# Keys and values of the second attention prepared in earlier stages, idle products in TensorE's waits, and a shorter clearing of mask rows

## The reference

```python
x = x + _L0_xattn_ref(_layernorm(x), ctx, ctx, mask, ...)     # attention
x = x + _L0_ffn_ref(_layernorm(x), ...)                       # mixture of experts
x = x + _L1_xattn_ref(ctx, _layernorm(x))                     # alignment by dynamic time warping
x = x + _L1_ffn_ref(_layernorm(x), ...)                       # gated, int weights
x = x + _L2_xattn_ref(_layernorm(x), ctx, Wq, Wkv, Wo)        # attention with rotary positions
x = x + _L2_ffn_ref(_layernorm(x), ...)                       # mixture of experts
x = x + _L3_xattn_ref(_layernorm(x), ctx, ctx, ..., 32)       # attention over the 32 largest scores
x = x + _L3_ffn_ref(_layernorm(x), g_info, ...)               # attention in two groups of tokens

def _rope(x):                     # in _L2_xattn_ref, on q and k
    ...
    x_rot = jnp.stack([-x[..., 1::2], x[..., 0::2]], axis=-1).reshape(x.shape)
    return x * cos + x_rot * sin
```

## Time and profile before

| | |
|---|---|
| median of 3 runs | 2571.38 us (2570.29 to 2576.07) |
| the profiled execution | 2571.94 us, its span 2570.2 us |
| busy | PE 2017.0 us (78%), DVE 1667.7 (65%), ACT 1114.9 (43%), POOL 1014.1 (39%) |
| stages, us | l0a 218.02, l0f 236.38, dtw 305.84, l1f 150.56, l2a 226.47, l2f 363.53, l3a 786.12, l3g 48.01, l3f 235.27 |
| l2a alone, busy | PE 154.17, DVE 157.64, ACT 86.78, POOL 104.14 |

### The profile page before, as it was taken

How to read it: one execution, slowest core, us unless ns; L and a number is a source line. 1 busy time by engine, 2 the same in 40 slices (tenths; PEclk the granted TensorE clock), 3 DMA queues, 4 the chain that set the end, 5 groups by cost and what they waited for, 6 DMA issues and landing times. The chain is left out here.

```text
span 2570.2 us, 39975 instructions
## 1 busy us (share of the span) xinstructions
PE 2017.0 (78%) x13076; PEld 1627.1 (63%) x13076; DVE 1667.7 (65%) x5397; ACT 1114.9 (43%) x3119; POOL 1014.1 (39%) x954
## 2 busy tenths in 40 slices
PE   7985898699659948865999937777777777756996
PEld 5664797599538835545999925555655555544664
DVE  5765111588972258843111179999999999976774
ACT  3552232455221115432333236666666766652443
POOL 3310453200000046503555436666666666634440
PEclk9996899655769979976999966666666757567998
DMA  2111565400210012123364230000000000000111
GB/s 91 64 55 60 215 242 183 127 21 1 82 37 1 1 46 71 59 71 134 131 211 157 85 113 9 1 9 9 1 9 9 1 1 1 1 7 26 46 55 66
DMA packets 91715, 161.09 MB, mean 63 GB/s; under 512 B 18494, under 2 KB 69847, under 8 KB 83543
## 3 DMA queue, kind: packets, MB, share of 16 engines
q0 software_dynamic: 23808, 85.50, 9.6%
q1 hardware_dynamic: 67704, 73.06, 9.0%
HBM read 194.38 MB, written 33.33 MB: 89 GB/s over the span
## 5 line engine op out<-in xcount | busy, mean ns | idle before, releaser
L555 DVE MATCH_REPLACE8 l3a_left<-l3a_top,l3a_left 128x256 f32<-128x256 f32 x768 | 307.4, 406 | 0.0
L548 DVE MAX8 l3a_top<-l3a_left 128x8 f32<-128x256 f32 x768 | 284.6, 411 | 0.0
L365 POOL TENSOR_TENSOR l3a_prob<-l3a_expd,l3a_rest 128x512 f32<-128x512 f32 x128 | 162.4, 1269 | 234.1 <-ACT l3a_rest L445 233.9
L270 PE MATMUL l3a_psT<-all_ident,l3a_prob 128*128 128x128 f32 x512 | 123.5, 387 | 162.7 <-POOL l3a_prob L365 162.7
L288 PE MATMUL l3a_psO<-l3a_probT,l3a_vp 128*128 128x128 f32 x1024 | 218.4, 380 | 28.8 <-ACT l3a_probT L461 28.8
L288 PEld LDWEIGHTS l3a_psO<-l3a_probT,l3a_vp 128*128 128x128 f32 x1024 | 187.7, 274 | 82.6 <-ACT l3a_probT L461 47.7
L270 PEld LDWEIGHTS l3a_psT<-all_ident,l3a_prob 128*128 128x128 f32 x512 | 83.9, 196 | 185.9 <-POOL l3a_prob L365 185.5
L445 ACT ACTIVATE l3a_rest<-l3a_left,l3a_nmax 128x256 f32<-128x256 f32 x256 | 116.1, 502 | 153.2 <-DVE l3a_left L555 152.5
L1485 ACT ACTIVATE l2f_hT<-l2f_psH,l2f_wt 128x128 f32<-128x128 f32 x312 | 89.0, 368 | 215.5 <-PE l2f_psH L1417 215.5
L352 POOL TENSOR_TENSOR l3a_kept<-l3a_raw_sc,l3a_mone 128x512 f32<-128x512 f32 x128 | 163.0, 1274 | 46.3 <-ACT l3a_raw_sc L429 45.8
L949 POOL TENSOR_SCALAR l2a_xn<-all_x,l2a_nmean,all_rstd 128x256 f32<-128x256 f32 x16 | 8.7, 554 | 433.3 <-DVE all_rstd L106 433.3
(11 more groups left out here) (533 smaller groups left out, 4723.9 us busy)
## 6 DMA issues: line engine op xcount, KB each, us to landing
o_at<-l0a_oraw SPq DMA_DIRECT2D x16, 256.0 KB, 2.0
l0a_osum<-o_at SPq DMA_DIRECT2D x32, 128.0 KB
kv_at<-dtw_kv SPq DMA_DIRECT2D x8, 512.0 KB, 2.8
o_at<-l2a_oraw SPq DMA_DIRECT2D x16, 256.0 KB, 2.0
l2a_osum<-o_at SPq DMA_DIRECT2D x32, 128.0 KB
l2f_yb<-rows_y SPq DMA_DIRECT2D x8, 512.0 KB, 7.3
o_at<-l3f_oraw SPq DMA_DIRECT2D x16, 256.0 KB, 2.0
l3f_osum<-o_at SPq DMA_DIRECT2D x32, 128.0 KB
```

What stands on the lines that cost most here:

```text
L270: mm = nc.tensor.transpose(psT[u % 2][:, kc, e, :], prob[:, u % 4, e, kc * P:kc * P + P], ident[:])
L365: nc.gpsimd.tensor_tensor(prob[:, u % 4, :, :], expd[:, u % 2, :, :], rest[:, u % 2, :, :], ALU.subtract).then_inc(picked, 1)
L548: ins = nc.vector.max(top[:, e, eight], rows[:, e, :] if r else scores[:, e, :])
L555: ins = nc.vector.match_replace(out=rows[:, e, :], in_to_replace=top[:, e, eight], in_values=rows[:, e, :] if r else scores[:, e, :], imm_ ...
```

## The change

- alignment (dtw) makes three products per batch: keys, keys with the columns of each pair exchanged (a third weight, the key weight with its columns permuted), and values. ACT writes the values straight between the ones of a vd buffer that POOL filled once. Keys and exchanged keys go to k_at (512 KB a batch), values with ones to the second half of kv_at (512 KB).
- gated_ffn (l1f): GpSimd loads both keys, multiplies them by cosine and sine, adds, makes the two parted copies and stores them in the first half of kv_at: five instructions a batch.
- l2a loads each batch's parted keys into k2 and values into vd, three buffers each, both 512 KB. load(b) for b of 3 and more stands ahead of realign(2(b - 2)). DVE exchanges q alone and copies no values; POOL turns and parts q alone; the memset of vd is gone there.
- keep_busy writes n idle products of the identity with 512 columns into a bank that is not yet in use, in front of a wait of PE: 2 + 2 in the head of l0a and l2a, 4 ahead of l2a's first scores, 1 before the last values and 8 before the last output product of l0a, l2a and l3f, 4 in each moe, 2 + 1 in l1f, 1 + 3 in l3g: 54 in all.
- stats.root(act, 1) stands behind read_q(0) and read_k(0). In l0a and l3f the memset of vd stands ahead of the second moments.
- find_groups: POOL clears one row set of 128x2048, and ACT copies it to the four parts of mrow, two ahead of its second root and two at its end.

The diff, cut to its core:

```diff
+def keep_busy(nc, out, ident, n):
+    for _ in range(n):
+        nc.tensor.matmul(out, ident[:], ident[:].unsqueeze(1).to_broadcast([P, 4, P]), start=True, stop=True)
...
                 if kv_at is not None:
-                    if b >= 2:
-                        sp.wait_ge(k2_set, b - 1)
-                        sp.wait_ge(v_ev, b - 1)
-                    of = kv_at[b].rearrange("p (w c n) -> p w c n", w=2, c=DC)
-                    sp.dma_start(kf[:, b % 2, :, :], of[:, 0]).then_inc(kv_in[b % 2], 16)
-                    sp.dma_start(vraw[:, b % 2, :, :], of[:, 1]).then_inc(kv_in[b % 2], 16)
+                    if b >= 3:
+                        sp.wait_ge(s2_done, 16 * (b - 2))
+                        sp.wait_ge(pv_ps, 2 * (b - 2))
+                    sp.dma_start(k2[:, b % 3, :, :, :].rearrange("p e c n -> p (e c n)"), kv_at[b, :, 0:4 * S]).then_inc(kv_in[b % 3], 16)
+                    sp.dma_start(vd[:, b % 3, :, :, :].rearrange("p t h m -> p (t h m)"), kv_at[b, :, 4 * S:]).then_inc(kv_in[b % 3], 16)
                     return
...
                 load(2)
+            if given and kv_at is None:
                 load(3)
             for y in range(2 * B):
-                if given and y % 2 == 0 and y // 2 + 4 < B:
+                if given and kv_at is None and y % 2 == 0 and y // 2 + 4 < B:
                     load(y // 2 + 4)
+                if kv_at is not None and y % 2 == 0 and 3 <= y // 2 + 2 < B:
+                    load(y // 2 + 2)
                 realign(y)
...
             def scores_1(n):
                 b, c, qt = n // 4, n % 4 // 2, n % 2
+                out = [take("s1", 4 * n + j) for j in range(4)]
+                if n == 0 and rope is not None:
+                    busy(out[0], 4)
                 if n % 4 == 0:
                     pe.wait_ge(qd_set, b + 1)
-                    pe.wait_ge(k2_set, b + 1)
-                out = [take("s1", 4 * n + j) for j in range(4)]
+                    if kv_at is None:
+                        pe.wait_ge(k2_set, b + 1)
+                    else:
+                        pe.wait_ge(kv_in[b % 3], 32 * (b // 3 + 1))
                 for e in (1, 0):
                     for j in range(4):
...
                 b, c = y // 2, y % 2
                 out = take("pv", y)
+                if y == 2 * B - 1:
+                    busy(out, 1)
                 pe.wait_ge(exp_done, 8 * (y + 1))
-                if c == 0:
...
             def out_project(b):
                 out = take("out", b)
+                if b == B - 1:
+                    busy(out, 8)
...
             q_parted(0)
-            k_parted(0)
+            if kv_at is None:
+                k_parted(0)
...
             read_x(0)
-            if stats is not None:
-                stats.root(act, 1)
             read_q(0)
             if kv_at is None:
                 read_k(0)
+            if stats is not None:
+                stats.root(act, 1)
...
+                nc.vector.memset(vd[:].rearrange("p b k h m -> p (b k h m)"), 1.0).then_inc(vd_one, 1)
+                dve.wait_ge(vd_one, 1)
             if x_in is not None:
                 dve.wait_ge(x_in[1], x_in[2])
             if stats is not None:
                 stats.moments(dve, 1)
-            nc.vector.memset(vd[:].rearrange("p b k h m -> p (b k h m)"), 1.0).then_inc(vd_one, 1)
-            dve.wait_ge(vd_one, 1)
             dve.wait_ge(q_in, 16 * n_q)
             if rope is not None:
-                exchange(0, 0, qf, q_ev, q_shuf, q_sin, q_turn)
...
             dve.wait_ge(w_in, 16 * n_w)
-            read_v(0)
+            if kv_at is None:
+                read_v(0)
...
                 if rope is not None and t == 1 and b + 1 < B:
-                    exchange(b + 1, 0, qf, q_ev, q_shuf, q_sin, q_turn)
-                if rope is not None and t == 2 and b + 1 < B:
-                    exchange(b + 1, 1, kf, k_ev if kv_at is None else None, k_shuf, k_sin, k_turn)
+                    exchange(b + 1)
                 if n < NQ:
                     row_max(n, (2, 3))
-                if t == 2 and b + 1 < B:
+                if t == 2 and b + 1 < B and kv_at is None:
...
+            keep_busy(nc, psX[:], ident, 4)
...
                     pe.wait_ge(a_again[i - 4], 16)
                 if i >= 2:
-                    pe.wait_ge(kv_ev, 2 * (i - 1))
-                for o in range(DC):
+                    pe.wait_ge(kv_ev, 3 * (i - 1))
+                for w in range(2):
+                    for o in range(DC):
+                        for c in range(DC):
+                            mm = nc.tensor.matmul((psT[i % 2][:, o * S:o * S + S] if w else psD[i % 2][:, o, :]),
+                                                  kv_sb[w][:, c, o * P:o * P + P], aT[:, b % 4, c, :],
+                                                  start=(c == 0), stop=(c == DC - 1))
+                    mm.then_inc(kv_ps, 1)
+                for t in range(QT):
                     for c in range(DC):
-                        mm = nc.tensor.matmul(psD[i % 2][:, o, :], kv_sb[0][:, c, o * P:o * P + P], aT[:, b % 4, c, :],
+                        mm = nc.tensor.matmul(psB[i % 2][:, t * D:t * D + D], aT[:, b % 4, c, t * P:t * P + P], kv_sb[2][:, c, :],
                                               start=(c == 0), stop=(c == DC - 1))
                 mm.then_inc(kv_ps, 1)
-                for t in range(QT):
...
-                act.wait_ge(kv_ps, 2 * i + 1)
-                nc.scalar.activation(kv[:, i % 2, 0, :, :], psD[i % 2][:], ACT.Copy).then_inc(kv_ev, 1)
-                act.wait_ge(kv_ps, 2 * i + 2)
-                nc.scalar.activation(kv[:, i % 2, 1, :, :].rearrange("p c n -> p (c n)"), psB[i % 2][:], ACT.Copy).then_inc(kv_ev, 1)
+                    act.wait_ge(kv_out[i % 2], 32 * (i // 2))
+                act.wait_ge(kv_ps, 3 * i + 1)
+                nc.scalar.activation(kx[:, i % 2, 0, :, :], psD[i % 2][:], ACT.Copy).then_inc(kv_ev, 1)
+                act.wait_ge(kv_ps, 3 * i + 2)
+                nc.scalar.activation(kx[:, i % 2, 1, :, :].rearrange("p c n -> p (c n)"), psT[i % 2][:], ACT.Copy).then_inc(kv_ev, 1)
+                act.wait_ge(kv_ps, 3 * i + 3)
+                if i == 0:
+                    act.wait_ge(vd_one, 1)
+                for t in range(QT):
+                    last = nc.scalar.activation(vd[:, i % 2, t, :, 0:DK],
+                                                psB[i % 2][:, t * D:t * D + D].rearrange("p (h d) -> p h d", d=DK), ACT.Copy)
+                last.then_inc(kv_ev, 1)
             act.wait_ge(e_read, 1)
...
+        @block.gpsimd
+        def _(pool):
+            pool.wait_ge(wave_in, 48)
+            for b in range(B):
+                pool.wait_ge(k_in[b % 2], 16 * (b // 2 + 1))
+                for w, wave in enumerate((cosT, sinT)):
+                    nc.gpsimd.tensor_tensor(kx[:, b % 2, w, :, :], kx[:, b % 2, w, :, :], wave[:].unsqueeze(1).to_broadcast([P, DC, S]),
+                                            ALU.mult).then_inc(k_waved, 1)
+                pool.wait_ge(k_waved, 2 * (b + 1))
+                nc.gpsimd.tensor_tensor(kx[:, b % 2, 0, :, :], kx[:, b % 2, 0, :, :], kx[:, b % 2, 1, :, :], ALU.add).then_inc(k_turned, 1)
+                pool.wait_ge(k_turned, b + 1)
+                if b >= 2:
+                    pool.wait_ge(k_out[b % 2], 16 * (b // 2))
+                for e in range(2):
+                    ins = nc.gpsimd.tensor_scalar(k2[:, b % 2, e, :, :], kx[:, b % 2, 0, :, :], even[:, e:e + 1], even[:, 2 + e:3 + e],
+                                                  ALU.mult, ALU.add)
+                ins.then_inc(k_parted, 1)
...
+                if not again:
+                    keep_busy(nc, psG[0][:], ident, 1)
...
+            keep_busy(nc, psG[0][:], ident, 2)
...
+            keep_busy(nc, psQ[0][:].rearrange("p t n -> p (t n)"), ident, 1)
...
+                if b == 0:
+                    keep_busy(nc, psQ[0][:].rearrange("p t n -> p (t n)"), ident, 3)
...
+            def clear(f, e):
+                nc.scalar.activation(mrow[:, f, e, :], zero[:], ACT.Copy)
...
+            act.wait_ge(z_set, 1)
+            clear(0, 0)
+            clear(0, 1)
             stats.root(act, 1)
...
             lengths(B - 1)
+            clear(1, 0)
+            clear(1, 1)
...
-            pool.wait_ge(m_zero, 1)
+            nc.gpsimd.memset(zero[:], 0.0).then_inc(z_set, 1)
```

More of the change, by code:

```diff
@@ L622, in paired_attention @@
         kvT = s.sb("kvT", [P, 2, DC, S]) if ctxT is not None else xnT
-        vraw = s.sb("vraw", [P, 2, QT, D]) if kv_at is not None else None
-        qf, kf = s.sb("qf", [P, 2, DC, S]), s.sb("kf", [P, 2, DC, S])
+        qf = s.sb("qf", [P, 2, DC, S])
+        kf = s.sb("kf", [P, 2, DC, S]) if kv_at is None else None
         qd, q2 = s.sb("qd", [P, 2, 2, DC, S]), s.sb("q2", [P, 2, 2, DC, S])
@@ L656, in paired_attention @@
         stored = s.sem("stored")
-        kv_in, o_out, o_in = ([s.sem(f"{n}{p}") for p in range(2)] for n in ("kv_in", "o_out", "o_in"))
```

(20 more changed lines are left out.)

105 lines of the change are left out of this document (59 added, 46 removed).

## The result

The changed kernel takes 2545.2 us (median of 4 runs, 2540.27 to 2550.27) against 2571.03 before (4 runs). The ratio is 0.9896, with a 95% interval of 0.9872 to 0.9919: faster by 1.0%, about half of what was forecast, and 5 us above the upper end of the range. The profiled execution has a span of 2548.4 us against 2570.2.

What follows compares the result with a forecast made beforehand. l2a was taken as bound by VectorE and by the order in which PE, DVE and POOL wait for each other. Stage terms summed to -48.8 us, from the median 2571.38 to 2522.6; range 2507 to 2540.

Steps and rivals of the forecast that it cites:

- The pace of l2a: l2a: a full batch takes 18.3 us instead of 20.85, with PE the longest engine and 1.7 us idle.
- the six periods: l2a, first transposed maxima of batch 0 to those of batch 6: 104.6 us instead of 126.0, so -21.4.
- nothing to spare. I count nothing, and keep the miss as a rival: l2a's loads: 4.3 us for store and reads plus 5.4 for loads equals the 9.7 available; counted as 0.
- rival B: Loads come late in l2a: batches 3 to 7 each wait 2 us (+10, 2533) or 4 us (2543); chance 0.17.
- The light batches: l2a's batches 1 and 2 lack inversion and output product: 5.2 us less over the periods, taken from l0a.
- The head of l2a: l2a's start: first scores 6.5 us earlier, then 5.8 less to the first transposes; -12.3 us (9 to 14).
- l0a's head: l0a's start: scores near 18.6, row maxima near 23.4 instead of 28.34; -4.9 us (up to -7.6).
- The tails: Last output product of l0a and l2a: 1.89 us instead of 3.75 after eight idle products; -1.9 each (0 to -2.7).
- l3f: l3f's tail: eight idle products outlast the 3.54 us wait and delay the last output product; +3.6 us.
- l1f: l1f: idle products speed the first gate and up, -2.2 us (0 without the clock); GpSimd's added turn costs 0.
- Rival F: l1f: POOL's turn holds some eight DVE scalings and normalisings up to 1.26 us each; +10, 2533; chance 0.05.
- l3g, dtw and the moes: l3g: shorter memset, faster queries, -5.0 us; dtw: added products and stores hidden, 0; two moe stages: -1.0 each.

## Why the prediction was wrong

**The pace of l2a: the work right, the total wrong.** 15.6 us of DVE was 15.9, 16.6 to 17.1 of PE was 16.8, the idle time of 1.7 was 1.5 and the batch of 18.3 was 18.3, once the loads were out of the way. (The 17.1 was put down in part to a lower clock, but its window in the earlier trace rows has a granted clock of 1.00; the work was simply close to 17.) l2a's miss of 29.8 us is 25.3 in the six periods, 1.3 in the last one, 3.4 in the tail and -0.2 in the head. Two terms failed in the periods, and one in the tail.

**The failed step: "nothing to spare. I count nothing, and keep the miss as a rival".** SP's queue in the changed kernel, and the scores that wait for it:

```profile
986.67 0.32 SPq L717 DMA_DIRECT2D o_at<-l2a_oraw  x1
988.68 1.07 SPq L723 DMA_DIRECT2D l2a_osum<-o_at  x2
989.85 0.42 SPq L705 DMA_DIRECT2D l2a_k<-kv_at  x1
990.31 0.43 SPq L706 DMA_DIRECT2D l2a_vd<-kv_at  x1
995.84 0.32 SPq L717 DMA_DIRECT2D o_at<-l2a_oraw  x1
998.43 1.08 SPq L723 DMA_DIRECT2D l2a_osum<-o_at  x2
```

```profile
997.91 1.16 PE L838 MATMUL l2a_bank<-l2a_k,l2a_qd 32*128 32x256 f32 x16 [2.75 <-DMA l2a_vd<-kv_at]
```

Both sides of the balance were off. The loads were put at 5.4 us, with 6.6 as the upper bound; they landed 5.8 and 6.9 us after issue, with the values issued 0.46 behind the keys, so 7.4. The store and the reads ahead of them were put at 4.3 and took 3.2. That is 10.6 in place of 9.7. And the time to spare was put at 9.7, but without the wait the scores of batch 4 would have started 995.16 - 986.67 = 8.5 us after the store. So the balance was not zero but short by 2. Every batch from 3 on missed by 2 to 4.7. Without load waits and stores held up the six periods take 112.5, with them 129.9: 17.4 us, of which 14.7 is waiting for the loads. The rest goes with slower products behind the waits: PE is busy 5.0 us longer in the six periods (102.8 against 97.8), a part of it in place of other waits. A step whose slack is worked out as zero should not have been counted with nothing: rival B had the right mechanism, and 3 us a batch, which is what was measured, would have made its time 2538. The prediction also saw only one side of SP's order. That loads directly ahead of a store are no better, since they hold the store, was shown by the two runs that tried it.

**The light batches.** "So 5.2 less" was taken from l0a. Six periods without reloads took 112.5, not 104.6. The two light periods took 18.5 and 19.8, 6.9 us more than was put, and the sixth 19.3, 1.0 more. That is 7.9 us, and 17.4 + 7.9 is the 25.3 by which the six periods missed. The light periods carry less work, but PE ran at a granted clock of 0.91 there. The clock is not all of it: with four buffers, split loads and no idle products the second light period ran at a granted clock of 1.00 and still took 18.35 us, with PE busy in 14.9; PE's waits were for the row maxima. In l0a the batches were bound by PE, so less work shortened them; in l2a the alternation of scores and maxima seems to set the pace. This is argued from the windows, not tested by a run. The last period took 18.3 us, where 17.8 - 0.8 was put.

**The head of l2a: right in sum.** -12.5 against -12.3, with both parts off by about 1 us in opposite directions.

**l0a's head: right, in part by luck.** The first scores at 18.31 (18.6), the first row maxima at 23.69 (23.4). The order of the readings did what was forecast, but the parted keys were ready at 17.28, and the scores then waited for the load of the output weights, which the sum did not have. The rows:

```profile
18.31 1.15 PE L838 MATMUL l0a_bank<-l0a_k,l0a_qd 32*128 32x256 f32 x16 [1.35 <-DMA l0a_wo<-in_L_wo]
...
23.50 3.75 PE L790 MATMUL l0a_bank<-l0a_xnT,l0a_wq 128*128 128x256 f32 x8 [4.05 <-ACT l0a_xnT L1072]
```

```profile
23.69 2.47 DVE L1185 TENSOR_REDUCE l0a_nm<-l0a_bank 128x2 f32<-128x512 f32 x4
```

Of the price of moving the root, one part was missed: behind it stands also the reading of batch 1's transposed x, so the next product waits 4.05 us for it and runs at the lower clock.

**The tails: the size of an idle product, and its effect.** At the higher level one costs 0.87 us (twelve in 10.46), not 0.95. Eight end 3.2 to 3.8 us before the wait does, and the product behind them took 3.78 in l0a and 3.59 in l2a: -1.9 each was not there. In l2a the time behind the last transposed maxima even grew by 1.5 us (38.9 to 40.4), which is the 3.4 above. With twelve, which reach to the end of the wait, the product took 1.99 and 1.89. The tail of the changed kernel's l2a:

```profile
1107.67 7.03 PE L81 MATMUL l2a_bank<-all_ident 128*128 128x512 f32 x16
1118.52 3.59 PE L790 MATMUL l2a_bank<-l2a_wo,l2a_oT 128*128 128x256 f32 x8 [3.82 <-POOL l2a_oT L1035]
```

**l3f: the sign right, the size not.** The idle products overshoot as forecast:

```profile
2534.76 7.11 PE L81 MATMUL l3f_bank<-all_ident 128*128 128x512 f32 x16
...
2541.70 1.89 PE L790 MATMUL l3f_bank<-l3f_wo,l3f_oT 128*128 128x256 f32 x8
```

All eight ran at the higher level, where a slow first one had been put, and the product ended 0.8 us later than before, counted from the stage's start, not 3.6. Over all profiles l3f took 234.9 to 236.6 us with idle products and 233.8 to 235.2 without.

**l1f.** The idle products stop 4.29 us before the weights are there, so the gate's product is still slow, and the up weights come later than before:

```profile
761.52 1.48 ACT L2250 ACTIVATE l1f_w_u<-l1f_raw_u 128x1536 f32<-128x1536 int32 x1 [5.24 <-DMA l1f_raw_u<-in_L_up]
...
763.14 3.52 PE L2208 MATMUL l1f_psG<-l1f_xnT,l1f_w_g 128*128 128x256 f32 x8 [4.29 <-ACT l1f_w_u L2250]
```

761.52 is 7.4 us from the barrier; before it was 6.3. In ten of the eleven other profiles of changed kernels, the second one of the same kernel among them, it is 6.3 to 6.6, and in one 7.5, so this is scatter of a load and hardly a cost of the change. Rival F, POOL's turn against DVE, is there in the groups by line of the changed kernel, and it is hidden:

```profile
L2265 DVE TENSOR_SCALAR l1f_xn<-all_x,all_mean,all_rstd 128x256 f32<-128x256 f32 (+1 forms) x16 | 9.2, 620 | 0.0
L2298 DVE TENSOR_SCALAR l1f_w_d<-l1f_raw_d 128x1536 f32<-128x1536 int32 x1 | 2.0, 2024 | 0.0
```

The sixteen normalising instructions took 406 ns on average before and 620 now, the scaling of the down weights 960 ns before and 2024 now, both beside POOL's work. The median stayed at 0.41 us and the longest took 1.42, so few of them were held, by about 1 us. PE's waits for DVE's copy of the transposed x sum to 8.1 us before and after. By the rule of the Trainium skill named in the prediction (SBUF — State Buffer, Who interferes with whom) they could be held for up to one POOL instruction each; the trace agrees (POOL's take 1.26 to 1.98 us), and no price on the path is seen.

**l3g, dtw and the moes.** In l3g the short memset no longer holds DVE (the instruction that took 5.02 us takes 0.17), and the two clears fit ahead of the root:

```profile
2271.27 1.80 POOL L2456 MEMSET l3g_zero<- 128x2048 f32 x1 [10.64 <-POOLq L59]
...
2276.02 3.69 ACT L2430 ACTIVATE groups_mrow<-l3g_zero 128x2048 f32<-128x2048 f32 x2
...
2281.26 1.99 PE L2381 MATMUL l3g_psQ<-l3g_wq,l3g_xT 128*128 128x256 f32 x8 [0.55 <-ACT l3g_xT L2416]
```

They took 3.69 us where 3.9 was put, and the stage gained 6.1 where 5.0 was. The three idle products did not overshoot, and the product behind them took 1.99 us for 3.78; the two runs without idle products put their worth in l3g at 2.3 to 2.7. dtw hid its added products (PE busy 252.8 us instead of 239.8) and its 8 MB of stores. l2f gained 1.8 for 1.0. l0f's 0.9 for 1.0 is no confirmation: the first expert's products took 5.37 us for 6.03, but the stage scatters by more than that.

## What to carry to other kernels

A transfer that must land within a wait is no free edit when the sum says "nothing to spare": work out its place in the queue, what stands ahead of it and behind it, and give it a buffer more, so that it can start a batch early. Where small round trips share the queue with large loads, put the loads right behind a round trip, one at a time if they can be split, and not directly ahead of a store whose read back is waited for. Idle products pay reliably only if they reach to the end of the wait; counts are to be set from the wait's length in the trace, stage by stage, and left out where the wait is shorter.

## What the runs showed of the hardware

512 KB loads took 5.8 us (keys) and 6.9 (values) to land in the change, where 256 KB had taken 2.9 and 3.3 before: twice the bytes, twice the time. They took 5.8 to 5.9 each when split, and only 4.4 and 5.3 where both stood directly ahead of a store. A store of 256 KB issued right behind 1 MB of loads had its read back issued 5.5 us after it instead of 2.0. Whether TensorE's clock holds over an idle gap of 3.2 to 3.4 us is not fixed: the same product behind nearly the same gap took 3.78 us in one execution (3.24) and 1.99 in another (3.40).
